# Layer norms by statistics operations, one tile at a time, and a staggered context norm

## The chip, the cores and the metric

The kernel runs on one core of a Trainium2 chip. The metric is the device time of one execution in microseconds. The kernel before was run three times: 4507.76, 4507.40 and 4503.47 us, with a median of 4507.4 us.

## The reference

Two layers of a gated cross-attention network on a residual `x` of 1024 rows of 128 features, with a context of 6404 rows of 128. Each layer adds a gated cross-attention and a gated mixture of eight experts. What matters for this change is where rows are normalised:

```python
def _layernorm(x, axis=-1, eps=1e-05):
    m = jnp.mean(x, axis=axis, keepdims=True)
    v = jnp.var(x, axis=axis, keepdims=True)
    return (x - m) / jnp.sqrt(v + eps)

# layer 0, cross-attention: context and latents are normalised once more inside
xn = layernorm(x, ln_x_g, ln_x_b)         # x here is the context, 6404 rows
ln = layernorm(latents, ln_l_g, ln_l_b)   # latents = _layernorm(residual)
# layer 1, cross-attention: the input and the output go through
def stable_layernorm(x, g):
    x = x / jax.lax.stop_gradient(jnp.max(x, axis=-1, keepdims=True))
    mean = jnp.mean(x, axis=-1, keepdims=True)
    var = jnp.mean(jnp.square(x - mean), axis=-1, keepdims=True)
    return (x - mean) * jax.lax.rsqrt(var + EPS) * g

x = x + tanh(g_xattn[0]) * xattn0(ctx, _layernorm(x))
x = x + tanh(g_ffn[0]) * experts0(_layernorm(x))
x = x + tanh(g_xattn[1]) * xattn1(_layernorm(x), ctx)
x = x + tanh(g_ffn[1]) * experts1(_layernorm(x))
```

## The kernel before

Rows lie on the 128 partitions, so the residual `X` is a tile of 128 x 8 x 128 (QT = 8 tiles of 128 rows), and the context `raw` (in the trace `a_ctx_rows`) is 128 x 51 x 128: 50 full tiles and one of 4 rows. A layer norm is then a reduction along the free axis within each partition. The program is a chain of blocks; every engine meets the others at the end of a block.

`layer_norm` (lines 119 to 130) handles T tiles at once on VectorE: a sum (L122), its division (L123), a subtraction of the mean with a broadcast operand (L124), a square (L125), a second sum (L126) and variance plus epsilon (L127). GpSimd raises that to the power -0.5 (`rstd`, L135), and VectorE multiplies by the result (L130). Each of these waits for the one before it through the semaphore `ln_step` or through the pair `var_ready` and `rstd_ready`. It is called for eight tiles in seven places: twice in the preparation of each attention layer, once behind the second attention, once in each mixture. Three more calls norm the context of layer 0, in parts of 17 tiles (`ln_parts`).

**The preparation of layer 0** is the block of lines 255 to 425. SyncE loads the context (L259, L261, semaphore `c_in`). VectorE norms the latents twice, tells TensorE by `lat_ready`, waits for the context (L359), then norms the three parts, with one `ctx_ready` behind each (L361 to L364). The rows are transposed in 16 jobs of up to four tiles: two for the latents, four for the tiles that need only the first part, four that need the second, six that need the third (the last two of these are of two tiles and of one). For each job TensorE transposes (L421), ScalarE applies gain and bias into `xt`, which has two buffers (L302, trace `a_x_new`), and copies to the rounded `hi` (L305, `a_x_hi`), and GpSimd subtracts to get `lo` (L330, `a_x_lo`). ScalarE may start job i only when `lo` of job i - 2 is done. GpSimd's queue is in a fixed order: it does the powers and the `lo` work by the calls of lines 332 to 340,

```python
rstd(pool, 17, var_ready, rstd_ready, 3)
lows(0, 2)
rstd(pool, 17, var_ready, rstd_ready, 4)
lows(2, 6)
rstd(pool, 17, var_ready, rstd_ready, 5)
lows(6, len(jobs))
```

The block ends when GpSimd's last `lo` is done; the next one begins with GpSimd's fills (L561 to L563).

**The preparation of layer 1** is the same code with another `hi` and `lo` path: ScalarE writes `hi` (L308), VectorE writes `lo` (L384, L387), and the context isn't normalised. VectorE norms the latents, divides by the row maximum (L354 to L356) and norms again. TensorE's jobs for the context wait for the same transfer `c_in` (L416).

**The mixtures** (`moe_layer`) begin with a layer norm of X (L1348), then TensorE transposes (L1392), ScalarE copies, and TensorE computes the gate's logits (L1397) once the expert weights are loaded (`w_in`, L1395). The wait at L1420 counts the steps of the norm.

The rest, about nine tenths of the span, is the main loops of the two attentions, which the change doesn't touch.

## Time and profile before

| | |
|---|---|
| the profiled execution's own time | 4508.5 us |
| span in its profile | 4506.7 us |
| runs | 4503.47, 4507.40, 4507.76 us |
| TensorE busy | 4199.3 us, 93% of the span |
| VectorE busy | 3411.4 us, 76% |
| ScalarE busy | 3192.4 us, 71% |
| GpSimd busy | 414.8 us, 9% |

The span is cut into stages by the blocks: preparation of layer 0 up to 86.2 us, the start of its attention to about 130 us, its loop to about 2300 us, the first mixture from 2322 to 2466 us, preparation of layer 1 to 2534 us, its loop to about 4428 us, the end of that attention to 4446 us and the second mixture to the end. Only the stretches outside the two loops contain layer norms. In them the engines wait for each other in turn, so that a timeline of one engine with its idle times tells which one the others wait for.

### The profile page before, as it was taken

How to read it: one execution, taken by the hardware profiler on the slowest of the kernel's cores; microseconds unless marked ns; L12 is line 12 of the kernel's file. 1: busy time of each engine (PE TensorE's matmuls, PEld its weight loads, DVE VectorE, ACT ScalarE, POOL GpSimd, SP SyncE). 2: the span in 40 equal slices, each digit the busy share in tenths (PEclk: the TensorE clock that was granted, in tenths of full speed). 3: DMA queues.
4: the chain of work that ended last, by engine and by line, in shares of the span. 5: the costliest groups of instructions: out<-in, count | busy, mean ns of one | idle time of the engine just before them, and what ended most of it. 6: DMA issues, size and time to landing. Idle time of an engine off the chain costs nothing. (4 is left out here: it accounts for less than half of the span.)

```text
span 4506.7 us, 75798 instructions
## 1 busy us (share of the span) xinstructions
PE 4199.3 (93%) x26651; PEld 2695.9 (60%) x26651; DVE 3411.4 (76%) x5067; ACT 3192.4 (71%) x5163; POOL 414.8 (9%) x348
## 2 busy tenths in 40 slices
PE   2999999999999999999978499999999999999995
PEld 1556666666666656666646366666666666666663
DVE  5788878787887888788752577777777777777785
ACT  2788888888888888888842367676766666666661
POOL 4111111111111111111100000000000000000000
PEclk9999999999999999999989599999999999999996
DMA  1000000000000000000010000000000000000000
GB/s 36 16 1 16 1 5 12 1 16 1 17 1 1 16 1 17 1 5 12 1 51 25 26 3 14 3 5 12 5 12 5 12 5 12 2 15 1 16 1 23
DMA packets 27285, 48.16 MB, mean 11 GB/s; under 512 B 9329, under 2 KB 18425, under 8 KB 24313
## 3 DMA queue, kind: packets, MB, share of 16 engines
q1 hardware_dynamic: 24824, 42.30, 2.8%
q8 instruction: 237, 3.88, 0.4%
q14 instruction: 158, 1.29, 0.1%
q10 hardware_dynamic: 2066, 0.69, 0.1%
HBM read 42.15 MB, written 0.82 MB: 10 GB/s over the span
## 5 line engine op out<-in xcount | busy, mean ns | idle before, releaser
L797 DVE TENSOR_TENSOR a_probs_lo<-a_probs 128x1024 fp32r<-128x1024 f32 x1764 | 2119.5, 1223 | 656.8 <-ACT a_probs L642 306.8
L638 ACT ACTIVATE a_probs<-scores_ps,a_c_bias,a_k_rstd 128x512 f32<-128x512 f32 x1892 | 1317.2, 776 | 35.9 <-PE scores_ps L1114 34.4
L1139 PE MATMUL out_ps<-a_probs_lo,a_v 128*128 128x512 f32 x3520 | 1135.6, 443 | 0.0
L1132 PE MATMUL out_ps<-a_probs,a_v 128*128 128x512 bf16 x3520 | 968.7, 391 | 37.7 <-DVE a_out_acc L810 27.7
L642 ACT ACTIVATE a_probs<-scores_ps,a_c_bias 128x1024 f32<-128x1024 f32 x818 | 870.4, 1112 | 115.6 <-PE scores_ps L1114 114.6
L1114 PE MATMUL scores_ps<-a_q_hi,a_k_hi 64*128 64x512 f32 x3528 | 793.6, 445 | 18.3 <-issue 9.4
L1139 PEld LDWEIGHTS out_ps<-a_probs_lo,a_v 128*128 128x128 f32 x3520 | 659.2, 188 | 220.4 <-issue 0.3
L1114 PE MATMUL scores_ps<-a_q_lo,a_k_hi 64*128 64x512 f32 x3528 | 703.4, 393 | 0.0
L1114 PE MATMUL scores_ps<-a_q_hi,a_k_lo 64*128 64x512 f32 x3528 | 699.2, 391 | 0.0
L1132 PEld LDWEIGHTS out_ps<-a_probs,a_v 128*128 128x128 f16 x3520 | 273.8, 97 | 590.8 <-issue 222.9
L607 ACT ACTIVATE a_v<-proj_ps 128x256 f16<-128x256 f32 x456 | 175.5, 385 | 519.2 <-PE proj_ps L1049 519.0
L1114 PEld LDWEIGHTS scores_ps<-a_q_hi,a_k_hi 64*128 64x128 f32 x3528 | 333.2, 184 | 209.1 <-issue 109.6
L569 POOL TENSOR_TENSOR a_k_rstd<-a_k_stat,minus_half 128x4 f32<-128x4 f32 x244 | 301.5, 1236 | 1698.5 <-DVE a_k_stat L774 1698.5
L1114 PEld LDWEIGHTS scores_ps<-a_q_lo,a_k_hi 64*128 64x128 f32 x3528 | 336.0, 185 | 76.0
L810 DVE TENSOR_TENSOR a_out_acc<-out_ps,a_out_acc 128x512 f32<-128x512 f32 x576 | 369.1, 682 | 11.4 <-PE out_ps L1139 11.4
L1114 PEld LDWEIGHTS scores_ps<-a_q_hi,a_k_lo 64*128 64x128 f32 x3528 | 335.6, 186 | 37.5
L618 ACT ACTIVATE a_k_hi<-proj_ps 128x256 fp32r<-128x256 f32 x454 | 175.2, 386 | 248.6 <-PE proj_ps L1057 248.1
L624 ACT ACTIVATE a_v<-a_v 128x512 fp32r<-128x512 f16 x454 | 283.9, 625 | 0.0
L1122 PE MATMUL spare_ps<-a_probs,a_v_last 128*32 128x512 bf16 x3520 | 283.1, 395 | 0.0
L1049 PE MATMUL proj_ps<-a_wkv_hi,a_x_hi 128*128 128x256 f32 x912 | 267.4, 293 | 14.7 <-ACT normed_T L675 6.9
L1049 PE MATMUL proj_ps<-a_wkv_lo,a_x_hi 128*128 128x256 f32 x912 | 258.9, 284 | 0.0
L1049 PE MATMUL proj_ps<-a_wkv_hi,a_x_lo 128*128 128x256 f32 x912 | 257.0, 282 | 0.0
(198 smaller groups left out, 3431.1 us busy)
## 6 DMA issues: line engine op xcount, KB each, us to landing
a_den<-a_inv_row SPq DMA_DIRECT2D x18, 1024.0 KB, 4.7
normed<-in_L_xattn_we_g SPq DMA_DIRECT2D x18, 256.0 KB, 2.8
a_wkv_raw<-in_L_xattn_wkv_g SPq DMA_DIRECT2D x18, 128.0 KB, 2.0
a_wo_raw<-in_L_xattn_wo_g SPq DMA_DIRECT2D x18, 128.0 KB, 2.0
m_w<-in_L_ffn_w1T SPq DMA_DIRECT2D x1, 2048.0 KB, 8.2
m_w<-in_L_ffn_w2T SPq DMA_DIRECT2D x1, 2048.0 KB, 12.6
a_wq_raw<-in_L_xattn_wq_g SPq DMA_DIRECT2D x18, 64.0 KB, 1.9
residual<-in_x SPq DMA_DIRECT2D x1, 512.0 KB, 3.8
```

Of the source, the lines that this page charges most:

```text
L569: nc.gpsimd.tensor_tensor(krs[:, par, 2 * j:2 * j + 2, :].rearrange("p t h -> p (t h)"), kst[:, 1, :], mhalf[:, 0:2 * GH], ALU.pow).then_i ...
L607: nc.scalar.activation(v16[:, par, 2 * j:2 * j + 2, :, 0:DH].rearrange("p t h d -> p (t h) d"), proj[:, 2 * P:4 * P].rearrange("p (a d) -> ...
L624: nc.scalar.activation(v32[:, par, 2 * j:2 * j + 2, :, :].rearrange("p t h k -> p (t h) k"), v16[:, par, 2 * j:2 * j + 2, :, :].rearrange( ...
L638: ins = nc.scalar.activation(probs[:, pb, e * 512:(e + 1) * 512], scores[:, b, e * 512:(e + 1) * 512], ACT.Exp, bias=cbias[:, tile:tile + ...
L642: ins = nc.scalar.activation(probs[:, pb, :], scores[:, b, :], ACT.Exp, bias=cbias[:, 1:2] if last else cbias[:, 0:1])
L797: nc.vector.tensor_tensor(plow[:, idx % NPL, :], probs[:, idx % NB, :], p_hi[:, idx % NB], ALU.subtract).then_inc(plo_ready, 1)
L810: ins = nc.vector.tensor_tensor(oacc[:, e, q], outs[:, e * 512:(e + 1) * 512], oacc[:, e, q], ALU.add)
L1049: last = nc.tensor.matmul(dst, a[:, x], w[:, :].rearrange("p (a c) -> p a c", a=2), start=t == 0 and m == 0, stop=m == 2, skip_group_check ...
L1114: last = nc.tensor.matmul(scores[:, b, e * 512:(e + 1) * 512], kk[r, c % 2, t, :], qq[r, n * 512:(n + 1) * 512], start=m == 0, stop=m == 2)
L1122: last = nc.tensor.matmul(last_ps[j:j + 32, :], vlast[:, c % 2, t, e, 4 - 4 * n:36 - 4 * n], p_hi[:, idx % NB, e * 512:(e + 1) * 512], sta ...
L1132: nc.tensor.matmul(outs[:, e * 512:(e + 1) * 512], v16[:, c % 2, t, e, :], p_hi[:, idx % NB, e * 512:(e + 1) * 512], start=t == 0, stop=False)
L1139: nc.tensor.matmul(outs[:, e * 512:(e + 1) * 512], v32[:, c % 2, t, e, :], plow[:, idx % NPL, e * 512:(e + 1) * 512], start=False, stop=t ...
```

## The change

Per tile, `bn_stats` gives six statistics of 128 values, `bn_aggr` makes mean and variance of them, and one `tensor_scalar` with two per-partition scalars subtracts the mean and multiplies by the power. The statistics lie in `few`, a part of `squares`, or for the context in `part`, a part of `a_ctx_sq`. `layer_norm` is now `ln_stats` followed by `ln_apply`. For the context the two are called apart: the statistics of part i + 1 come ahead of the application to part i. GpSimd's order changes with that: the second power comes ahead of the latents' two jobs, the third right behind them.

```diff
-        def layer_norm(dve, step, x, dst, sq, T, var_ready, rstd_ready, n):
-            shape = [P, T, D]
-            step(nc.vector.tensor_reduce(stat[:, 0, 0:T], x, AX.X, ALU.add))
-            step(nc.vector.tensor_scalar(stat[:, 1, 0:T], stat[:, 0, 0:T], 1.0 / D, None, ALU.mult))
-            step(nc.vector.tensor_tensor(dst, x, over(stat[:, 1, 0:T], shape), ALU.subtract))
-            step(nc.vector.tensor_tensor(sq, dst, dst, ALU.mult))
-            step(nc.vector.tensor_reduce(stat[:, 2, 0:T], sq, AX.X, ALU.add))
-            nc.vector.tensor_scalar(stat[:, 3, 0:T], stat[:, 2, 0:T], 1.0 / D, LN_EPS,
-                                    ALU.mult, ALU.add).then_inc(var_ready, 1)
-            dve.wait_ge(rstd_ready, n)
-            step(nc.vector.tensor_tensor(dst, dst, over(stat[:, 0, 0:T], shape), ALU.mult))
+        few = sqz[:, :, :].rearrange("p t d -> p (t d)")[:, 0:8 * QT].rearrange("p (t k) -> p t k", k=8)
+
+        def ln_stats(dve, step, x, a, b, part, var_ready):
+            for t in range(a, b):
+                nc.vector.bn_stats(part[:, t, 0:6], x[:, t, :]).then_inc(step.sem, 1)
+            step.n += b - a
+            dve.wait_ge(step.sem, step.base + step.n)
+            for t in range(a, b):
+                nc.vector.bn_aggr(part[:, t, 6:8], part[:, t, 0:6]).then_inc(step.sem, 1)
+            step.n += b - a
+            dve.wait_ge(step.sem, step.base + step.n)
+            nc.vector.tensor_scalar(stat[:, 3, a:b], part[:, a:b, 7], LN_EPS, None, ALU.add).then_inc(var_ready, 1)
+
+        def ln_apply(dve, step, x, dst, a, b, part, rstd_ready, n):
+            dve.wait_ge(rstd_ready, n)
+            for t in range(a, b):
+                nc.vector.tensor_scalar(dst[:, t, :], x[:, t, :], part[:, t, 6:7], stat[:, 0, t:t + 1],
+                                        ALU.subtract, ALU.mult).then_inc(step.sem, 1)
+            step.n += b - a
+            dve.wait_ge(step.sem, step.base + step.n)
+
+        def layer_norm(dve, step, x, dst, T, var_ready, rstd_ready, n):
+            ln_stats(dve, step, x, 0, T, few, var_ready)
+            ln_apply(dve, step, x, dst, 0, T, few, rstd_ready, n)
...
                     if L == 0:
-                        rstd(pool, 17, var_ready, rstd_ready, 3)
+                        rstd(pool, 17, var_ready, rstd_ready, 3, 0)
+                        rstd(pool, 17, var_ready, rstd_ready, 4, 17)
                         lows(0, 2)
-                        rstd(pool, 17, var_ready, rstd_ready, 4)
-                        lows(2, 6)
-                        rstd(pool, 17, var_ready, rstd_ready, 5)
-                        lows(6, len(jobs))
+                        rstd(pool, 17, var_ready, rstd_ready, 5, 34)
+                        lows(2, len(jobs))
...
                     if L == 0:
+                        part = sq[:, :, :].rearrange("p t d -> p (t d)")[:, 0:(CTX_FULL + 1) * 8].rearrange("p (t k) -> p t k", k=8)
+                        def normed(i):
+                            a, b = ln_parts[i]
+                            ln_apply(dve, step, raw, raw, a, b, part, rstd_ready, 3 + i)
+                            dve.sem_inc(ctx_ready, 1)
                         for i, (a, b) in enumerate(ln_parts):
-                            layer_norm(dve, step, raw[:, a:b, :], raw[:, a:b, :], sq[:, 0:b - a, :], b - a,
-                                       var_ready, rstd_ready, 3 + i)
-                            dve.sem_inc(ctx_ready, 1)
+                            ln_stats(dve, step, raw, a, b, part, var_ready)
+                            if i:
+                                normed(i - 1)
+                        normed(len(ln_parts) - 1)
...
-                                pe.wait_ge(step_s, 6 + 1)
+                                pe.wait_ge(step_s, 3 * QT + 1)
```

VectorE in the preparation of layer 0, the context's part of the order before; `stat` holds sums, means, variances and powers:

```order
L122 TENSOR_REDUCE stat<-a_ctx_rows 128x17 [waits a0_ln_step,a0_ctx_in]
L123 TENSOR_SCALAR stat<-stat 128x17 [waits a0_ln_step]
L124 TENSOR_TENSOR a_ctx_rows<-a_ctx_rows,stat 128x2176 [waits a0_ln_step]
L125 TENSOR_TENSOR a_ctx_sq<-a_ctx_rows 128x2176 [waits a0_ln_step]
L126 TENSOR_REDUCE stat<-a_ctx_sq 128x17 [waits a0_ln_step]
L127 TENSOR_SCALAR stat<-stat 128x17 [waits a0_ln_step]
L130 TENSOR_TENSOR a_ctx_rows<-a_ctx_rows,stat 128x2176 [waits a0_rstd_ready]
L122 TENSOR_REDUCE stat<-a_ctx_rows 128x17 [waits a0_ln_step]
```

and what stands there now:

```order
L124 BN_STATS a_ctx_sq<-a_ctx_rows 128x6 [waits a0_ln_step,a0_ctx_in]
L124 BN_STATS a_ctx_sq<-a_ctx_rows 128x6 x16
L128 BN_AGGR a_ctx_sq<-a_ctx_sq 128x2 [waits a0_ln_step]
L128 BN_AGGR a_ctx_sq<-a_ctx_sq 128x2 x16
L131 TENSOR_SCALAR stat<-a_ctx_sq 128x17 [waits a0_ln_step]
L124 BN_STATS a_ctx_sq<-a_ctx_rows 128x6 x17
L128 BN_AGGR a_ctx_sq<-a_ctx_sq 128x2 [waits a0_ln_step]
L128 BN_AGGR a_ctx_sq<-a_ctx_sq 128x2 x16
L131 TENSOR_SCALAR stat<-a_ctx_sq 128x17 [waits a0_ln_step]
L137 TENSOR_SCALAR a_ctx_rows<-a_ctx_rows,a_ctx_sq,stat 128x128 [waits a0_rstd_ready]
L137 TENSOR_SCALAR a_ctx_rows<-a_ctx_rows,a_ctx_sq,stat 128x128 x16
```

The application to the first part (L137) now stands behind the statistics of the second, and only the first instruction of each group waits.

GpSimd in the same block before (`a_x_lo` is the `lo` of a job):

```order
L135 TENSOR_TENSOR stat<-stat,minus_half 128x17 [waits a0_var_ready]
L330 TENSOR_TENSOR a_x_lo<-a_x_new,a_x_hi 128x512 [waits a0_xh_done] x2
L135 TENSOR_TENSOR stat<-stat,minus_half 128x17 [waits a0_var_ready]
L330 TENSOR_TENSOR a_x_lo<-a_x_new,a_x_hi 128x512 [waits a0_xh_done] x4
L135 TENSOR_TENSOR stat<-stat,minus_half 128x17 [waits a0_var_ready]
L330 TENSOR_TENSOR a_x_lo<-a_x_new,a_x_hi 128x512 [waits a0_xh_done] x8
```

and now:

```order
L149 TENSOR_TENSOR stat<-stat,minus_half 128x17 [waits a0_var_ready] x2
L344 TENSOR_TENSOR a_x_lo<-a_x_new,a_x_hi 128x512 [waits a0_xh_done] x2
L149 TENSOR_TENSOR stat<-stat,minus_half 128x17 [waits a0_var_ready]
L344 TENSOR_TENSOR a_x_lo<-a_x_new,a_x_hi 128x512 [waits a0_xh_done] x12
L344 TENSOR_TENSOR a_x_lo<-a_x_new,a_x_hi 128x256 [waits a0_xh_done]
```

All work on the context's jobs now stands behind the third power; before, four jobs stood ahead of it.

## Rows read from the trace of the kernel before

**Rows 1.** The page's busy part, the whole span: engine, busy us, share, instructions

```profile
PE 4199.3 (93%) x26651; PEld 2695.9 (60%) x26651; DVE 3411.4 (76%) x5067; ACT 3192.4 (71%) x5163; POOL 414.8 (9%) x348
```

**Rows 2.** Windows: stretch, its us, busy us (instructions), PEclk, DMA share, GB/s

```profile
0.00:91.50 91.50, 16.22 (x60) 10.93 (x60) 59.00 (x47) 23.00 (x37) 43.18 (x39) 1.00 0.17 45
...
200.00:700.00 500.00, 488.92 (x3146) 308.33 (x3145) 405.36 (x614) 424.24 (x747) 78.15 (x61) 1.00 0.02 8
```

**Rows 3.** Timeline of VectorE, the first layer norm: start us, us, operation [idle before]

```profile
6.24 1.22 DVE L122 TENSOR_REDUCE stat<-residual 128x8 f32<-128x1024 f32 x1 [6.24 <-PEq L97]
...
11.49 0.17 DVE L127 TENSOR_SCALAR stat<-stat 128x8 f32<-128x8 f32 x1
...
13.51 1.23 DVE L130 TENSOR_TENSOR normed<-normed,stat 128x1024 f32<-128x1024 f32 x1 [1.85 <-POOL stat L135]
...
14.77 1.22 DVE L122 TENSOR_REDUCE stat<-normed 128x8 f32<-128x1024 f32 x1
```

**Rows 4.** VectorE on the context: the first reductions, ns min/median/max, and the last operation's timeline row

```profile
L122 DVE TENSOR_REDUCE stat<-a_ctx_rows x3: 2421/2421/2421, 23.3 to 57.3; 128x17 f32<-128x2176 f32 x3
...
71.73 3.47 DVE L130 TENSOR_TENSOR a_ctx_rows<-a_ctx_rows,stat 128x2176 f32<-128x2176 f32 x1 [3.18 <-POOL stat L135]
```

**Rows 5.** Timeline of GpSimd in the first stage's second half

```profile
53.63 5.94 POOL L330 TENSOR_TENSOR a_x_lo<-a_x_new,a_x_hi 128x512 fp32r<-128x512 f32 x3
...
68.64 3.06 POOL L135 TENSOR_TENSOR stat<-stat,minus_half 128x17 f32<-128x17 f32 x1 [7.49 <-DVE stat L127]
...
77.91 2.61 POOL L330 TENSOR_TENSOR a_x_lo<-a_x_new,a_x_hi 128x512 fp32r<-128x512 f32 x2 [0.33 <-ACT a_x_hi L305]
...
83.57 1.95 POOL L330 TENSOR_TENSOR a_x_lo<-a_x_new,a_x_hi 128x512 fp32r<-128x512 f32 x2 [0.23 <-ACT a_x_hi L305]
...
85.75 0.45 POOL L330 TENSOR_TENSOR a_x_lo<-a_x_new,a_x_hi 128x128 fp32r<-128x128 f32 x1 [0.23 <-ACT a_x_hi L305]
```

**Rows 6.** Windows at the end of the two context transfers, columns as in rows 2

```profile
20.50:21.00 0.50, 0.00 (x0) 0.00 (x0) 0.00 (x0) 0.00 (x0) 0.50 (x1) 1.00 0.23 55
...
21.00:21.50 0.50, 0.00 (x0) 0.00 (x0) 0.00 (x0) 0.00 (x0) 0.50 (x1) 1.00 0.01 4
...
2483.00:2483.50 0.50, 0.00 (x0) 0.00 (x0) 0.30 (x2) 0.00 (x0) 0.09 (x1) 0.50 0.30 95
...
2485.00:2486.00 1.00, 0.00 (x0) 0.00 (x0) 0.92 (x1) 0.00 (x0) 0.05 (x1) 0.50 0.04 12
```

**Rows 7.** Timeline of VectorE, small operations and one that reads one tensor

```profile
90.75 0.29 DVE L815 TENSOR_TENSOR a_wkv_lo<-a_wkv_raw,a_wkv_hi 128x128 fp32r<-128x128 f32 x1 [0.58 <-ACT a_wkv_hi L649]
...
90.96 0.29 DVE L816 SCALAR_TENSOR_TENSOR a_wkv_lo<-a_wkv_raw,a_wkv_hi 128x128 fp32r<-128x128 f32 x1
...
4461.94 0.64 DVE L1353 MAX8 m_top<-m_logit 128x8 f32<-128x8 f32 x8
...
4468.84 1.12 DVE L1382 SCALAR_TENSOR_TENSOR residual<-proj_ps,m_combine,residual 128x128 f32<-128x128 f32 x4 [2.15 <-PE proj_ps L1427]
...
2317.77 0.75 DVE L1244 TENSOR_SCALAR branch<-branch,a_cols 128x1024 f32<-128x1024 f32 x1 [0.32 <-PEq L508]
...
84.95 0.62 DVE L374 TENSOR_SCALAR a_rows<-a_rows 128x64 f32<-128x64 f32 x1
```

**Rows 8.** One line's instructions in the main loop: ns min/median/max

```profile
L797 DVE TENSOR_TENSOR a_probs_lo<-a_probs x1764: 1207/1225/1295, 128.7 to 4405.6; 128x1024 fp32r<-128x1024 f32 x196
```

**Rows 9.** Timeline of TensorE after the first layer's mixture norm

```profile
2336.26 0.99 PE L1397 MATMUL proj_ps<-m_wg,normed_T 128*128 128x8 f32 x4 [3.08 <-DMA m_w<-in_L_ffn_w2T]
```

**Rows 10.** Timeline of TensorE, transposes of the second layer's preparation

```profile
2486.42 1.97 PE L421 MATMUL scores_ps<-identity,normed 128*128 128x128 f32 x8 [12.01 <-DVEq L358]
...
2489.29 1.09 PE L421 MATMUL scores_ps<-identity,a_ctx_rows 128*128 128x128 f32 x4 [0.91 <-DVE a_ln_lo L384]
```

**Rows 11.** The last norm: a window as in rows 2, and TensorE's row

```profile
4450.00:4451.00 1.00, 0.00 (x0) 0.00 (x0) 0.97 (x2) 0.00 (x0) 0.00 (x0) 0.50 0.00 0
...
4458.07 3.58 PE L1397 MATMUL proj_ps<-m_wg,normed_T 128*128 128x8 f32 x16 [1.11 <-ACT normed_T L1333]
```

More of the change, by code:

```diff
@@ L132, in rstd @@
-        def rstd(pool, T, var_ready, rstd_ready, n):
+        few = sqz[:, :, :].rearrange("p t d -> p (t d)")[:, 0:8 * QT].rearrange("p (t k) -> p t k", k=8)
[9 more added lines that the diff above has]
+            nc.vector.tensor_scalar(stat[:, 3, a:b], part[:, a:b, 7], LN_EPS, None, ALU.add).then_inc(var_ready, 1)
@@ L134, in rstd @@
+        def rstd(pool, T, var_ready, rstd_ready, n, a=0):
             pool.wait_ge(var_ready, n)
-            nc.gpsimd.tensor_tensor(stat[:, 0, 0:T], stat[:, 3, 0:T], mhalf[:, 0:T],
+            nc.gpsimd.tensor_tensor(stat[:, 0, a:a + T], stat[:, 3, a:a + T], mhalf[:, 0:T],
                                     ALU.pow).then_inc(rstd_ready, 1)
@@ L350, in _ @@
                     step = Steps(dve, ln_step)
-                    layer_norm(dve, step, X[:, :, :], Z[:, :, :], sqz[:, :, :], QT, var_ready, rstd_ready, 1)
+                    layer_norm(dve, step, X, Z, QT, var_ready, rstd_ready, 1)
                     if L == 1:
@@ L356, in _ @@
                         step(nc.vector.tensor_tensor(Z[:, :, :], Z[:, :, :], over(stat[:, 1, 0:QT], [P, QT, D]), ALU.mult))
-                    layer_norm(dve, step, Z[:, :, :], Z[:, :, :], sqz[:, :, :], QT, var_ready, rstd_ready, 2)
+                    layer_norm(dve, step, Z, Z, QT, var_ready, rstd_ready, 2)
                     dve.sem_inc(lat_ready, 1)
```

8 lines of the change are left out of this document (4 added, 4 removed).

## The prediction

> **What bounds the kernel now.** The busy part of the page comes first [rows 1]: TensorE is at 93%, so in most of the span a faster VectorE can bring nothing. The windows then show where that doesn't hold [rows 2]: in 500 us of a main loop TensorE is busy for 489, in the first 91.5 us for 16, with VectorE at 59. Layer norms lie only in such stretches. So the question for each norm is whether VectorE ends the wait there. I read that from the timelines, norm by norm.
>
> A norm of eight tiles takes 14.77 - 6.24 = 8.53 us [rows 3]: five large operations of 1.22, two small ones of 0.17 to 0.19, 1.85 of waiting for GpSimd's power, and about 0.03 between operations. The other six run alike, at about 8.45. In the first layer's preparation the context's part starts at 23.3, ends at 71.73 + 3.47 = 75.20 [rows 4], and the stage ends with GpSimd's last `lo` at 86.20 [rows 5]. Whatever ends that `lo` earlier shifts all that follows.
>
> **The price of the new operations.** No row shows a statistics operation, so I bound each by the nearest rows [rows 7].
> - BN_STATS reads 128 columns of one tensor. Two independent operations of 128 columns start 0.21 apart and last 0.29. I take 0.21 for each and 0.29 for the last. Ends: 0.15 if it used a second read port, 0.34 if the program passed twice over the 128 columns (0.21 plus 128/1024 of about 1.07, the share of 1.22 that grows with the columns).
> - BN_AGGR reads six numbers. MAX8 on eight columns takes 0.64 for eight, 0.08 each. I take that, since it's the row with about as many columns. Ends: 0.05, and 0.17, which a lone small operation like L127 lasts [rows 3].
> - The new TENSOR_SCALAR has one SBUF tensor as input. L1244, of that form, takes 0.75 for 1024 columns where two-input operations take 1.22 [rows 3], so for 128 columns it saves about 0.06: 0.15 apart, 0.25 for the last. Ends: 0.08 (MAX8) and 0.26 (L1382, four in 1.12).
>
> Here a rule speaks against the change. In the trace, L816 starts 0.21 after L815, which lasts 0.29: independent operations overlap, which many small ones need [rows 7]. The Trainium skill (VectorE: DVE Perf Modes, The DRAIN you can't avoid) says that an operation does not start until the pipe of the one before is empty, and advises few operations; the trace disagrees for independent ones. What it would give here is the first rival.
>
> **A norm of eight tiles afterwards.** Statistics 7 x 0.21 + 0.29 = 1.76; aggregation 0.64; the addition of epsilon 0.17; two gaps 0.08; the way to GpSimd and back about 1.80, unchanged; application 7 x 0.15 + 0.25 = 1.30; gap 0.03. Sum 5.78, so 2.7 less than 8.45.
>
> **Part by part, against the profiled execution's own 4508.5 us.**
> 1. *Latents of layer 0.* The two norms end at 6.24 + 2 x 5.78 = 17.8 instead of about 23.2. But VectorE then needs the context, and its transfer still moves 55 GB/s up to 21.0 and 4 behind that [rows 6]. I take 20.9. Three microseconds of the gain turn into a wait for the transfer.
> 2. *Context of layer 0.* For 17 tiles: statistics 16 x 0.21 + 0.29 = 3.65, aggregation 17 x 0.08 = 1.36, epsilon 0.18, gaps 0.11, in all 5.3. The third `var_ready` of the context comes behind three such groups and one application (16 x 0.15 + 0.25 + 0.05 = 2.7), at 20.9 + 15.9 + 2.7 = 39.5. The first two powers lie under statistics; the third, 3.06 plus 0.08 to start [rows 5], doesn't, and all `lo` work of the context is queued behind it. It starts at 42.6. From 77.91 to 83.57 GpSimd starts four full `lo`, 1.415 each, paced together with ScalarE and its two buffers, and from the start of the last full one to the end there are 86.20 - 83.57 = 2.63 [rows 5]. Twelve full jobs: 42.6 + 11 x 1.415 + 2.63 = 60.8.
> 3. *The shared port.* The application to the last part runs beside `lo` work. The trace shows that this hurts: L374, a one-input operation on 64 columns, takes 0.62 beside a `lo`, twice what L815 needs for 128 [rows 7], and L130 on the context 3.47 where the operations of the same size take 2.42 [rows 4]. Statistics should be spared, since the third reduction, at 57.3 beside `lo` work, kept the 2.42 of the other two [rows 4, 5]. If the 17 applications and the `lo` simply exclude each other, GpSimd loses up to 17 x 0.15 = 2.6, some of it in pauses that it has anyway; I take half, 1.3. The stage ends at 62.1 instead of 86.2: **24.1 us**.
> 4. *Mixture of layer 0.* After its norm TensorE waits 3.08 us for the expert weights [rows 9], and their transfer starts with the block. A norm shorter by 2.7 only lengthens that wait: **0**. If this cover were missing, it would be 2.7 more.
> 5. *Preparation of layer 1.* Two norms, 5.4. The latents' transposes move from 2486.42 to 2481.0 and the context's from 2489.29 to 2483.9 [rows 10]; the context's transfer is thinning out by then, 95 GB/s at 2483 and 12 at 2485 [rows 6]. Between a loss of 0 and of 2 I take 0.4, since little is left at 2483.5: **5.0**.
> 6. *Norm behind the second attention.* Nothing beside it: **2.7**.
> 7. *Mixture of layer 1.* Its weights have landed before 4450 (0 GB/s in that window), and TensorE needs them at 4458.07 - 2.7, measured against a block that starts earlier by as much [rows 11]: **2.7**.
>
> Sum 24.1 + 0 + 5.0 + 2.7 + 2.7 = 34.5, so 4508.5 - 34.5 = 4474.0; the median shown lies 1.1 below the profiled execution, hence 4472.9, rounded to **4473**.
>
> **Rivals.**
> - *Small operations don't overlap.* Each pays its whole length: 0.29, 0.17 and 0.25 per tile. The eight-tile norm takes 7.75 and gains 0.7; the latents end at 21.7; a context part takes 17 x 0.46 + 0.29 = 8.1, an application 4.3, the third `var_ready` comes at 50.3, the power ends at 53.5 and the stage, by the 19.5 from there of part by part 2 and 3, at 73.0. Gain 13.2 + 1.4 + 0.7 + 0.7 = 16.0: 4491. For it: statistics operations may be built otherwise than MAX8. Against it: L815 and L816 overlap, and so do eight MAX8 in 0.64. Chance 0.13.
> - *GpSimd starves the last application.* The Trainium skill (SBUF — State Buffer, SBUF: two separate sides) calls the port an exclusive lock held for the whole instruction; L374 and L130 agree [rows 4, 7]. Worked out from rows: if one application gets through per `lo` and a third in the pause of each pair, 12 are done when eight `lo` are (42.6 + 8 x 1.415 = 53.9), the rest at 54.7. From VectorE's last context operation to the end of the stage were 86.20 - 75.20 = 11.0, so it ends at 65.7 instead of 62.1: gain 30.9, time 4476.5. Chance 0.12. The powers don't act so: L797 never exceeds 1295 ns among 1764, though GpSimd's powers run among them [rows 8].
> - *Slower.* The statistics operation is a long program, several passes over the tile at a slow rate. On the path lie 51 tiles of the context and 32 of the later norms, 83 in all. The gain of 34.5 is used up at 0.42 more per tile, that is where statistics and aggregation together cost 0.71 instead of 0.29. At 0.85 they add 46 there and some 6 more in the latents, past the wait: 18 slower, 4525. Against it: the rows on 128 columns last 0.29, and four of L1382 take 1.12. Chance 0.03.
> - *The gain is taken back.* Everything behind the first stage shifts by 24 us; something that doesn't shift (a transfer, TensorE's granted clock at the start of a loop) eats most of it. The loops' loads are issued inside them and shift too. Chance 0.03, about 4500.
>
> **How the numbers follow.** The forecast has 0.69. Its own spread: statistics at 0.15 give 83 x 0.06 = 5 more, no port loss 1.3 and no late transfer 0.4, thus 4466; statistics at 0.26, aggregation at 0.10 and applications at 0.20 cost 4.2 + 1.7 + 2.5 = 8.4, thus 4481. The starved case lies inside; the range reaches to the first rival's 4491 and down to 4465. A measurement here tells 0.2%, 9 us, from no change: all three first cases are faster by more. Faster 0.94, same 0.03, slower 0.03.
>
> **What would show it.** In the profile afterwards: BN_STATS groups of 17 lasting 3.7 us and BN_AGGR groups 1.4; VectorE idle for about 3 us before the context, released by the transfer; one power between statistics and the `lo` run, which starts near 42 and ends near 62; applications of 2.6 us for parts one and two and a much longer one for part three; the wait for the expert weights in the first mixture grown to 5.8; the norms at 5.8 elsewhere. BN_STATS lasting 0.4 or more each, a stage end behind 70, or loops that are longer than before would make the forecast wrong.

## The result, and the profile after

The changed kernel takes 4482.4 us (median of six runs, 4479.22 to 4483.43) where the kernel before takes 4506.8 (median of six, 4503.47 to 4507.76): a ratio of 0.9946, with a 95% interval from 0.9936 to 0.9956. The gain by medians is 24.4 us; 34.5 were forecast. The changed kernel's profiled execution took 4479.22, 3.2 below its median, and that of before 4508.5, 1.7 above its median, so 4.9 of the 29.3 by which the two profiles differ belong to these two executions and not to the change.

The page's busy part, beside [rows 1]:

```profile
PE 4194.4 (94%) x26651; PEld 2692.1 (60%) x26651; DVE 3394.0 (76%) x5328; ACT 3191.6 (71%) x5163; POOL 408.7 (9%) x348
```

VectorE is busy for 17 us less and TensorE for 5 less: most of what shrank is time in which TensorE waited.

VectorE's timeline (start us, us, operation, idle time before it) begins with one norm of eight tiles, which answers to [rows 3], and then shows the context's three parts, which answer to [rows 4]:

```profile
6.25 1.65 DVE L124 BATCH_NORM_STATS2 squares<-residual 128x6 f32<-128x128 f32 x8 [6.25 <-PEq L97]
7.93 0.64 DVE L128 BATCH_NORM_AGGREGATE squares<-squares 128x2 f32<-128x6 f32 x8
...
10.63 2.14 DVE L137 TENSOR_SCALAR normed<-residual,squares,stat 128x128 f32<-128x128 f32 x8 [1.86 <-POOL stat L149]
12.80 1.64 DVE L124 BATCH_NORM_STATS2 squares<-normed 128x6 f32<-128x128 f32 x8
```

```profile
21.90 3.38 DVE L124 BATCH_NORM_STATS2 a_ctx_sq<-a_ctx_rows 128x6 f32<-128x128 f32 x17 [2.67 <-DMA a_ctx_rows<-in_ctx]
25.32 1.23 DVE L128 BATCH_NORM_AGGREGATE a_ctx_sq<-a_ctx_sq 128x2 f32<-128x6 f32 x17
...
31.44 6.47 DVE L137 TENSOR_SCALAR a_ctx_rows<-a_ctx_rows,a_ctx_sq,stat 128x128 f32<-128x128 f32 x17
38.06 3.39 DVE L124 BATCH_NORM_STATS2 a_ctx_sq<-a_ctx_rows 128x6 f32<-128x128 f32 x17
...
42.84 7.56 DVE L137 TENSOR_SCALAR a_ctx_rows<-a_ctx_rows,a_ctx_sq,stat 128x128 f32<-128x128 f32 x17
50.55 9.48 DVE L137 TENSOR_SCALAR a_ctx_rows<-a_ctx_rows,a_ctx_sq,stat 128x128 f32<-128x128 f32 x17 [0.15 <-DVE a_ctx_rows L137]
```

A norm takes 12.80 - 6.25 = 6.55 us, where it took 8.53. Its statistics and aggregation cost what was expected (1.65 and 0.64), its application 2.14 instead of 1.30. The context starts at 21.90, behind a wait of 2.67 for the transfer. Statistics of 17 tiles take 3.38 and aggregation 1.23, but the same 17 applications take 6.47, then 7.56, then 9.48.

GpSimd beside them, to compare with [rows 5]:

```profile
34.67 2.65 POOL L344 TENSOR_TENSOR a_x_lo<-a_x_new,a_x_hi 128x512 fp32r<-128x512 f32 x2
43.00 3.12 POOL L149 TENSOR_TENSOR stat<-stat,minus_half 128x17 f32<-128x17 f32 x1 [5.68 <-DVE stat L131]
46.06 2.70 POOL L344 TENSOR_TENSOR a_x_lo<-a_x_new,a_x_hi 128x512 fp32r<-128x512 f32 x2
...
53.24 2.61 POOL L344 TENSOR_TENSOR a_x_lo<-a_x_new,a_x_hi 128x512 fp32r<-128x512 f32 x2 [1.58 <-ACT a_x_hi L319]
...
62.88 2.60 POOL L344 TENSOR_TENSOR a_x_lo<-a_x_new,a_x_hi 128x512 fp32r<-128x512 f32 x2 [4.21 <-ACT a_x_hi L319]
...
69.21 0.46 POOL L344 TENSOR_TENSOR a_x_lo<-a_x_new,a_x_hi 128x128 fp32r<-128x128 f32 x1 [0.23 <-ACT a_x_hi L319]
```

The third power starts at 43.00 (39.6 was forecast), the `lo` run behind it at 46.06 (42.6), and the stage ends at 69.67 (62.1) instead of 86.20. In the run there are two pauses that the forecast didn't have, 1.58 and 4.21. ScalarE's and TensorE's rows for the second pause:

```profile
61.36 0.78 ACT L316 ACTIVATE a_x_new<-scores_ps,a_cols 128x512 f32<-128x512 f32 x1 [4.03 <-PE scores_ps L442]
```

```profile
60.14 1.97 PE L442 MATMUL scores_ps<-identity,a_ctx_rows 128*128 128x128 f32 x8 [5.08 <-DVEq L379]
```

The transposes for part three wait for VectorE's last application, which ended at 60.03. Behind the first stage two rows answer to [rows 9] and to the norms elsewhere:

```profile
2316.60 3.55 PE L1418 MATMUL proj_ps<-m_wg,normed_T 128*128 128x8 f32 x16 [5.23 <-DMA m_w<-in_L_ffn_w2T]
```

```profile
4410.74 1.64 DVE L124 BATCH_NORM_STATS2 squares<-normed 128x6 f32<-128x128 f32 x8
...
4417.21 1.23 DVE L1280 TENSOR_TENSOR normed<-normed,a_rows 128x1024 f32<-128x1024 f32 x1
```

TensorE's wait for the expert weights grew from 3.08 to 5.23, and the norm behind the second attention takes 4417.21 - 4410.74 = 6.47 instead of about 8.45.

The stages against each other, in us (the first loop begins with VectorE's fill of `spare_ps`, here called the loop's start):

| stage | before | after | gain | forecast |
|---|---|---|---|---|
| preparation of layer 0, to the loop's start | 89.6 | 73.1 | 16.5 | 24.1 |
| loop's start to the first mixture | 2233.1 | 2229.8 | 3.3 | 0 |
| first mixture | 144.0 | 145.2 | -1.2 | 0 |
| preparation of layer 1, to its loop | 71.1 | 67.6 | 3.5 | 5.0 |
| second loop, with the norm behind it | 1908.7 | 1904.7 | 4.0 | 2.7 |
| second mixture | 60.2 | 57.1 | 3.1 | 2.7 |

The gains add up to the spans' difference, 29.3, within rounding. Of the last two the norms themselves account for 2.0 each. The first row is far above scatter: a second profile of the changed kernel (e11 below) has 73.07. The preparation of layer 1 is clear of it too (71.1 and in e2 71.3 with the old operations, 67.2 to 69.3 in all kernels with the new statistics). In the loops and mixtures kernels that share their code differ by 2 to 4 us, as much as the gains shown there.

### The profile page after: what moved, and what is told of

It is laid out like the page before. It is cut to its first block and busy times, and to the rows that moved or that the text cites. A ratio compares the mean times of both kernels' runs of the same rounds, so it can differ in the third digit from the quotient of the medians.

```text
span 4477.4 us, 76059 instructions
## 1 busy us (share of the span) xinstructions
PE 4194.4 (94%) x26651; PEld 2692.1 (60%) x26651; DVE 3394.0 (76%) x5328; ACT 3191.6 (71%) x5163; POOL 408.7 (9%) x348
## 3 DMA queue, kind: packets, MB, share of 16 engines
q14 instruction: 163, 1.33, 0.1%
```

## Experiments

All stage times come from each kernel's one profiled execution; medians of the whole kernel scatter by some 2 us. What separates the variants is the loop's start: 89.63 before, 73.10 after. The first theory: the forecast's mechanism holds, and what it missed is one price (the application) and one contention (`lo` against application). The rivals: the order brings the gain by itself, or the operations do; the loops changed.

**The change's two halves (e1, e2).** In e1 the order is the old one:

```diff
                         for i, (a, b) in enumerate(ln_parts):
                             ln_stats(dve, step, raw, a, b, part, var_ready)
-                            if i:
-                                normed(i - 1)
-                        normed(len(ln_parts) - 1)
+                            normed(i)
```

with GpSimd's calls as before (power, `lows(0, 2)`, power, `lows(2, 6)`, power, `lows(6, ...)`).

> The new operations everywhere, but the context's three parts one after the other as in the kernel before (statistics, power, application of a part before the next part's statistics; the `lo` work between the powers). Theory A (the shortfall lies in the application's own cost of 0.257 us per tile, and in the `lo` work that starves it): a part takes 4.8 for statistics, 3.2 for the power and 4.5 for the application; parts end at 34.4, 46.9 and, since the third power waits for four `lo`, about 60 to 62; six full `lo` are left after the third power, two of which can run beside the application, so the preparation ends at 69 to 71, where the changed kernel has 69.7: the stagger by itself is worth about nothing. Whole kernel within 3 us of the changed one, about 4483. Rival B (the stagger carries the gain, as 'all lo work behind one power' was forecast to end at 62): without it three powers of 3.1 stand open instead of one, the preparation ends at 76 or later, and the kernel takes about 4490.

It took 4492.4 us (six runs; ratio to before 0.997, 0.9957 to 0.9982). The last `lo` ended at 79.02, the loop started at 82.45: rival B. VectorE's rows show why:

```profile
29.68 6.36 DVE L137 TENSOR_SCALAR a_ctx_rows<-a_ctx_rows,a_ctx_sq,stat 128x128 f32<-128x128 f32 x17 [3.17 <-POOL stat L149]
...
44.23 8.48 DVE L137 TENSOR_SCALAR a_ctx_rows<-a_ctx_rows,a_ctx_sq,stat 128x128 f32<-128x128 f32 x17 [3.17 <-POOL stat L149]
...
60.90 8.48 DVE L137 TENSOR_SCALAR a_ctx_rows<-a_ctx_rows,a_ctx_sq,stat 128x128 f32<-128x128 f32 x17 [3.17 <-POOL stat L149]
```

Each application stands behind an open power (3.17), and the two later ones have four `lo` beside them and take 8.48. I had let them run free.

The kernel e2 has the old operations in the new order (`ln_stats` with two reductions, division, subtraction and square of 17 tiles, `ln_apply` with one wide product).

> The old operations (reductions and wide two-input operations) in the new, staggered order. Theory A: statistics of a part 10.3, so parts at 33.6 and 43.9, application 2.4 or more, third variance at about 57 to 59, third power until 60 to 63, ten full `lo` behind it: 60.1 + 9 x 1.415 + 2.63 = 75.5 to 78; 8 to 11 less than the 86.2 of before, so 4496 to 4499 in all, nothing gained elsewhere. Rival B (order is worth nothing by itself with either kind of operation): preparation at 84 to 87, kernel 4505 to 4508.

4501.9 us (ten runs; ratio 0.999, 0.998 to 1.0), last `lo` at 82.57, loop's start at 86.00, between the two forecasts. The order alone gives 3.6 us, the operations alone 7.2, both together 16.5. GpSimd's rows show what lies between 75.5 and 82.57:

```profile
33.55 3.06 POOL L144 TENSOR_TENSOR stat<-stat,minus_half 128x17 f32<-128x17 f32 x1 [11.70 <-DVE stat L130]
43.66 5.17 POOL L144 TENSOR_TENSOR stat<-stat,minus_half 128x17 f32<-128x17 f32 x1 [7.05 <-DVE stat L130]
48.80 6.87 POOL L339 TENSOR_TENSOR a_x_lo<-a_x_new,a_x_hi 128x512 fp32r<-128x512 f32 x2
57.29 5.16 POOL L144 TENSOR_TENSOR stat<-stat,minus_half 128x17 f32<-128x17 f32 x1 [1.62 <-DVE stat L130]
62.42 5.88 POOL L339 TENSOR_TENSOR a_x_lo<-a_x_new,a_x_hi 128x512 fp32r<-128x512 f32 x3
```

The same power takes 3.06 beside VectorE's reduction and 5.17 beside wide two-input operations; two `lo` take 6.87 instead of 2.5. So the third power ends at 62.45, where the lower forecast had 60.1 (2.3 us), and the first three `lo` behind it take 5.88 beside the last wide application instead of 3.9 (2.0). The rest, 2.8, is a slip of the expectation: it counted ten full `lo` behind the third power, and in this order there are twelve. Staggering lays the powers beside wide operations, unless the operations are replaced too; that explains at least part of why the halves add up to less than the whole.

**What a `lo` does to an application (e3).**

```diff
                         rstd(pool, 17, var_ready, rstd_ready, 5, 34)
+                        pool.wait_ge(ctx_ready, 3)
                         lows(2, len(jobs))
```

> The changed kernel, but GpSimd's `lo` work from the third on waits until VectorE has ended the last application. Theory A (a `lo` holds VectorE's operations back): the second and third application take 4.5 each (0.257 x 17 + 0.1), as the first does where no `lo` runs, instead of 7.56 and 9.48; the third ends near 55, and the preparation ends at about 55 + 9 x 1.415 + 2.63 = 70 or a bit more, since ten `lo` follow. Rival (the later applications are slow for another reason, such as operands written by GpSimd or a slower VectorE): they still take 7 to 9 and the preparation ends at 74 or later.

```profile
31.22 6.48 DVE L137 TENSOR_SCALAR a_ctx_rows<-a_ctx_rows,a_ctx_sq,stat 128x128 f32<-128x128 f32 x17
...
42.62 4.44 DVE L137 TENSOR_SCALAR a_ctx_rows<-a_ctx_rows,a_ctx_sq,stat 128x128 f32<-128x128 f32 x17
47.20 4.44 DVE L137 TENSOR_SCALAR a_ctx_rows<-a_ctx_rows,a_ctx_sq,stat 128x128 f32<-128x128 f32 x17
```

Theory A: the second and third application take 4.44, and the first, which still has two `lo` beside it, 6.48. The last `lo` ended at 69.88, so to hold the `lo` work back gains nothing over letting it starve the applications: what the applications win, the `lo` work loses, as it waits for them. The 70 of the expectation was met by luck: the third application ended at 51.64 instead of near 55, and twelve full `lo` follow it instead of ten, 51.78 + 11 x 1.415 + 2.63 = 70.0. One run: 4485.8 us. Windows of the changed kernel say it in small: stretch, its us, the busy us and number of applications that lie in it at least in part, PEclk, DMA share, GB/s.

```profile
33.50:34.60 1.10, 1.10 (x6) 1.00 0.00 0
34.70:36.00 1.30, 1.30 (x2) 1.00 0.00 0
34.86:36.04 1.18, 1.18 (x1) 1.00 0.00 0
51.70:53.20 1.50, 1.50 (x8) 1.00 0.00 0
```

The counts take in those that an edge of the window cuts. Beside a power (until 34.67) the applications go on at their own pace, 0.256 apart, as in the pause from 51.66. From 34.86 to 36.04, beside one `lo`, a single one lies open; the second of the row above had started before the `lo` and was ending. So one application gets through per `lo`, 1.28 after the one before instead of 0.256, and is open for the length of the `lo`, the longest 1411 ns. Each `lo` beside applications costs them 1.28 - 0.256 = 1.02 us, and that gives the lengths of the groups: 4.44 + 2 x 1.02 = 6.48 for the first (6.47 measured), three `lo` 7.5 (7.56), five 9.5 (9.48), and four in e1 8.5 (8.48).

**The price of the application (e4).** The mean and the power are replaced by two constants, so this kernel leaves the normalisation's subtraction and factor out:

```diff
-                nc.vector.tensor_scalar(dst[:, t, :], x[:, t, :], part[:, t, 6:7], stat[:, 0, t:t + 1],
+                nc.vector.tensor_scalar(dst[:, t, :], x[:, t, :], 0.01, 0.99,
                                         ALU.subtract, ALU.mult).then_inc(step.sem, 1)
```

> The application in every norm with two constants instead of the tile's mean and power read from memory: the mean's subtraction and the power's factor are left out of the result. Theory A1 (0.257 apart is the price of the two scalars read from memory before the columns): with constants the operations start 0.15 to 0.20 apart and last 0.25 to 0.29, the eight-tile application takes 1.3 to 1.6 instead of 2.14, and each later norm is 0.5 to 0.9 shorter. Rival A2 (the price is that of any one-input, two-operation instruction on 128 columns in float32): still 0.25 apart, 2.1 for eight.

```profile
10.56 1.17 DVE L137 TENSOR_SCALAR normed<-residual 128x128 f32<-128x128 f32 x8 [1.85 <-POOL stat L149]
...
31.52 2.40 DVE L137 TENSOR_SCALAR a_ctx_rows<-a_ctx_rows 128x128 f32<-128x128 f32 x17
...
42.15 9.94 DVE L137 TENSOR_SCALAR a_ctx_rows<-a_ctx_rows 128x128 f32<-128x128 f32 x17 [0.89 <-POOL stat L149]
```

```profile
39.01 3.10 POOL L149 TENSOR_TENSOR stat<-stat,minus_half 128x17 f32<-128x17 f32 x1 [1.74 <-DVE stat L131]
...
61.25 0.46 POOL L344 TENSOR_TENSOR a_x_lo<-a_x_new,a_x_hi 128x128 fp32r<-128x128 f32 x1 [0.22 <-ACT a_x_hi L319]
```

Eight take 1.17 and seventeen 2.40, hence (2.40 - 1.17) / 9 = 0.137 apart, where the real ones take (4.44 - 2.14) / 9 = 0.256: reading two scalars per partition from memory costs 0.12 us per instruction here. That is A1, below even its 0.15 to 0.20, and it shows more: with an application near the 0.15 that the forecast had taken, the third power ends at 42.1 (42.6 forecast) and the stage at 61.7 (62.1 forecast). One run: 4472.3 us (4473 forecast). The third application still took 9.94 beside `lo` work, so whether an application is held off has nothing to do with its scalars. But here the second application had ended at 41.25, before the `lo` run began; only one stands beside it instead of two. From the third power's end to the last `lo` the stage needs 19.6; in e3, with no application beside the `lo` run, it needs 69.88 - 51.78 = 18.1. One starved application thus costs the end 1.5.

**The application by wide operations (e5).**

```diff
-            for t in range(a, b):
-                nc.vector.tensor_scalar(...)
+            step(nc.vector.tensor_tensor(dst[:, a:b, :], x[:, a:b, :], over(part[:, a:b, 6], shape), ALU.subtract))
+            step(nc.vector.tensor_tensor(dst[:, a:b, :], dst[:, a:b, :], over(stat[:, 0, a:b], shape), ALU.mult))
```

> The application of every norm as two wide two-input operations (subtract the means, multiply by the powers) in place of one operation per tile; statistics and order as in the change. Theory A (per-tile operations with two scalars cost 0.257 each, wide ones 1.22 per eight tiles and 2.42 per 17): the eight-tile application takes 2.5 instead of 2.14, so each of the four later norms is 0.3 to 0.4 longer; 17 tiles take 4.9 where no `lo` runs instead of 4.45. Beside `lo` a wide operation was held by about 1 us only (3.47 for 2.42), where 17 small ones take 7.6 to 9.5: so the second and third application take 5 to 7, and the preparation ends at 66 to 69 instead of 69.7; whole kernel the same within 2 us. Rival B (one instruction per tile is the better form even beside `lo`): the preparation ends at 70 to 74 and the kernel is 2 to 5 slower than the changed one.

```profile
46.53 3.47 DVE L137 TENSOR_TENSOR a_ctx_rows<-a_ctx_rows,a_ctx_sq 128x2176 f32<-128x2176 f32 x1 [0.49 <-POOL stat L147]
50.04 3.37 DVE L138 TENSOR_TENSOR a_ctx_rows<-a_ctx_rows,stat 128x2176 f32<-128x2176 f32 x1
```

```profile
31.53 5.17 POOL L147 TENSOR_TENSOR stat<-stat,minus_half 128x17 f32<-128x17 f32 x1 [1.71 <-DVE stat L131]
...
41.33 5.17 POOL L147 TENSOR_TENSOR stat<-stat,minus_half 128x17 f32<-128x17 f32 x1 [2.14 <-DVE stat L131]
46.47 9.28 POOL L342 TENSOR_TENSOR a_x_lo<-a_x_new,a_x_hi 128x512 fp32r<-128x512 f32 x4
```

4484.1 us (four runs), the last `lo` at 68.54: theory A, 1.1 earlier than in the change, which the median doesn't show. Two instructions lose one stretch of about 1 us each to a `lo`, where seventeen lose many; in return both powers beside the wide operations take 5.17, and four `lo` 9.28. Wide operations and `lo` hold each other off. With the power it is one-sided: beside the second power (31.53 to 36.70) a wide operation runs from 33.82 to 36.25 in its usual 2.42, while the power waits.

**The order once more (e6).** All three statistics ahead of all applications; on GpSimd the latents' two `lo`, then three powers, then the rest:

> All three statistics of the context first, then the three applications; on GpSimd the two `lo` of the latents before the first power, then the three powers, then all `lo` of the context. Theory A (the loss in the changed kernel is that the third part's tiles are applied last, after the third power, and beside `lo` work that starves them, so ScalarE waits 4.0 for part three): statistics end at 36.2, the third power at 39.3, the first application runs free until 40.8, GpSimd's context work starts near 43.9 and is never without input again, twelve full `lo` later the preparation ends at 61.5 to 64. Kernel 4474 to 4477. Rival B (VectorE and GpSimd share one port and the work on it is what counts, whatever the order): the preparation ends at 67 or later. Rival C (statistics first is worse, since the first `lo` of the context starts 0 to 3 later): 70.

```profile
36.18 4.44 DVE L137 TENSOR_SCALAR a_ctx_rows<-a_ctx_rows,a_ctx_sq,stat 128x128 f32<-128x128 f32 x17
40.77 8.60 DVE L137 TENSOR_SCALAR a_ctx_rows<-a_ctx_rows,a_ctx_sq,stat 128x128 f32<-128x128 f32 x17 [0.15 <-DVE a_ctx_rows L137]
49.52 8.60 DVE L137 TENSOR_SCALAR a_ctx_rows<-a_ctx_rows,a_ctx_sq,stat 128x128 f32<-128x128 f32 x17 [0.15 <-DVE a_ctx_rows L137]
```

4479.7 us (four runs), the last `lo` at 67.76: rival B, and theory A's 61.5 to 64 failed. The first application is free (4.44), the other two take 8.60 each; GpSimd stood still twice for 3.18, before 52.21 and 60.97. What it gained over the change, 1.9, is about what e10 gets by moving the latents' `lo` alone; the rest of the order only moves the loss about.

**The `lo` subtractions on VectorE (e7)**, between its own operations (`lows_v(0, 2)` behind the second statistics, `lows_v(2, 4)` behind the second application, the rest at the end), GpSimd with the powers alone:

> The first preparation's `lo` subtractions on VectorE instead of GpSimd, placed between its statistics and applications; GpSimd has only the powers. Theory A (applications are slow because a GpSimd `lo` holds VectorE off): all three applications take 4.4 to 4.5; a `lo` of 512 columns takes VectorE 0.6 to 0.7; the third application ends at 52.5, and from there ScalarE's two activations per job (1.33) set the pace: end at 64 to 66, 4 to 6 less than in the change. Rival B (applications slow in themselves from the second on): 7.6 and 9.5 again, end at 72 or later.

```profile
32.56 4.44 DVE L137 TENSOR_SCALAR a_ctx_rows<-a_ctx_rows,a_ctx_sq,stat 128x128 f32<-128x128 f32 x17
...
47.72 4.44 DVE L137 TENSOR_SCALAR a_ctx_rows<-a_ctx_rows,a_ctx_sq,stat 128x128 f32<-128x128 f32 x17
...
54.50 0.69 DVE L383 TENSOR_TENSOR a_x_lo<-a_x_new,a_x_hi 128x512 fp32r<-128x512 f32 x1 [0.91 <-ACT a_x_hi L319]
...
65.39 0.29 DVE L383 TENSOR_TENSOR a_x_lo<-a_x_new,a_x_hi 128x128 fp32r<-128x128 f32 x1 [0.26 <-ACT a_x_hi L319]
```

Theory A in each number: applications of 4.44, `lo` of 0.69 (GpSimd needs 1.3), ScalarE's pace of 1.33 from 54.50 on, the end at 65.68. The loop's start moved only from 73.10 to 70.83, since the small operations on `a_rows` and `a_cols`, which had stood under cover of GpSimd's work, now come behind the last `lo`; the median of four runs, 4482.1, shows no gain.

**The transfer (e8)**, in layer 0 alone; layer 1 keeps its one transfer and its wait:

```diff
-                    sp.dma_start(raw[:, 0:CTX_FULL, :], ...).then_inc(c_in, 16)
+                    for s, (a, b) in zip((c_first, c_second, c_in), ((0, 17), (17, 34), (34, CTX_FULL))):
+                        sp.dma_start(raw[:, a:b, :], ...).then_inc(s, 16)
...
-                    dve.wait_ge(c_in, 32)
...
+                            dve.wait_ge(*((c_first, 16), (c_second, 16), (c_in, 32))[i])
                             ln_stats(dve, step, raw, a, b, part, var_ready)
```

> The context's transfer of layer 0 in three transfers with a semaphore each, so that VectorE's statistics of part one wait for part one alone. Theory A (the 2.67 us that VectorE waits for the transfer lie on the path): statistics start at 19.2 to 19.4, everything behind moves by 2.5, the preparation ends at 67.0 to 67.5, kernel 2.5 less than the changed one. Rival B (the parts land together, since the queues work on all of them at once, or later parts then come late): the first part lands at 21 or later, the end is within 1 of 69.7.

```profile
19.38 3.38 DVE L124 BATCH_NORM_STATS2 a_ctx_sq<-a_ctx_rows 128x6 f32<-128x128 f32 x17
```

The statistics follow the latents' norm without a wait, the last `lo` ends at 67.10, and the median of four runs is 4478.6: theory A.

**One move (e10).** GpSimd's latents' `lo` ahead of the first power:

```diff
+                        lows(0, 2)
                         rstd(pool, 17, var_ready, rstd_ready, 3, 0)
                         rstd(pool, 17, var_ready, rstd_ready, 4, 17)
-                        lows(0, 2)
                         rstd(pool, 17, var_ready, rstd_ready, 5, 34)
```

> The changed kernel with one thing moved: GpSimd does the two `lo` of the latents before the context's first power instead of after the second. Theory A (a `lo` beside an application costs what the applications lose): the first application, with no `lo` beside it, takes 4.44 instead of 6.47, the third statistics, the third power and the second application start 2.0 earlier, and the preparation ends 1.5 to 2.0 earlier: last `lo` at 67.7 to 68.2. Rival B (the two `lo` only stand elsewhere in the same chain, since from the second application on GpSimd's `lo` and the applications exclude each other and the sum is the same): end within 0.5 of 69.7.

```profile
31.33 4.45 DVE L137 TENSOR_SCALAR a_ctx_rows<-a_ctx_rows,a_ctx_sq,stat 128x128 f32<-128x128 f32 x17
```

The first application takes 4.45, all behind it comes 2.1 earlier, the last `lo` ends at 67.54, and the kernel takes 4478.4 us (five runs): theory A, a little more than its 67.7 to 68.2. So a `lo` beside statistics cost nothing, and beside an application it cost 1.0.

**All together (e9, e9b).** The transfer in parts, the latents' `lo` first, three statistics, and then, for every group of four tiles, its applications and VectorE's own `lo` of the group two before:

```diff
+                        for i in range(2, len(jobs)):
+                            a, b = jobs[i][1][0], jobs[i][1][-1] + 1
+                            dve.wait_ge(rstd_ready, 2 + sum(b > c for c, d in ln_parts))
+                            for t in range(a, b):
+                                ins = nc.vector.tensor_scalar(raw[:, t, :], raw[:, t, :], part[:, t, 6:7], stat[:, 0, t:t + 1],
+                                                              ALU.subtract, ALU.mult)
+                                ins.then_inc(step.sem, 1)
+                            step.n += b - a
+                            dve.wait_ge(step.sem, step.base + step.n)
+                            dve.sem_inc(ctx_ready, 1)
+                            if i >= 4:
+                                low_v(i - 2)
...
-                            pe.wait_ge(ctx_ready, 1 + sum(tiles[-1] >= b for a, b in ln_parts))
+                            pe.wait_ge(ctx_ready, i - 1)
```

The small operations on rows and columns went ahead of the last `lo`.

> All that helped, put together: the context's transfer in three parts, the latents' two `lo` on GpSimd first, all three statistics, then the applications by groups of four tiles (one job of the transposes each) with the context's `lo` subtractions between them on VectorE, two groups behind. Theory (VectorE's own work is then the bound, with no operation stretched): 19.4 + 3 x 4.78 = 33.7, then 51 applications and 13 drains of about 0.12 (14.8) and 12 `lo` of 0.66 with two short ones (8.7): last `lo` at 57 to 60, first instruction of the loop (VectorE's memset) at 61 to 64 where the changed kernel has 73.1; kernel 9 to 12 less than the changed one, 4471 to 4474. Rival (ScalarE's two activations per job, 1.33, or their two buffers become the bound, with the `lo` waiting for them): last `lo` at 62 or later.

4474.0 us (five runs; ratio 0.9927, 0.9913 to 0.994), the last `lo` at 60.03, at the upper end of the theory, the loop's start at 63.56. In the second form a group's last application signals `ctx_ready` itself, and the wait for `step.sem` goes:

> As e9_interleaved, but a group's last application signals TensorE itself, and VectorE goes on without waiting for it. If the bound is VectorE's own work, 13 waits of about 0.1 go: 1.0 to 1.5 earlier than e9_interleaved. If ScalarE paces the groups, no difference.

```profile
38.56 1.11 DVE L400 TENSOR_SCALAR a_ctx_rows<-a_ctx_rows,a_ctx_sq,stat 128x128 f32<-128x128 f32 x4
39.59 0.69 DVE L394 TENSOR_TENSOR a_x_lo<-a_x_new,a_x_hi 128x512 fp32r<-128x512 f32 x1
...
57.74 0.29 DVE L394 TENSOR_TENSOR a_x_lo<-a_x_new,a_x_hi 128x128 fp32r<-128x128 f32 x1
```

```profile
34.10:58.10 24.00, 13.82 (x52) 8.65 (x52) 22.28 (x73) 18.10 (x28) 3.09 (x1) 0.66 0.00 1
```

4472.1 us (five runs; ratio to before 0.9925, 0.9912 to 0.9939), 10 less than the change by medians; the loop starts at 61.56, 11.5 earlier than in the change. Between the third statistics and the end VectorE is busy for 22.28 of 24.00 us (the third column of busy times, behind TensorE's two), so it is the bound, and no operation is stretched. The 13 waits cost 2.0, more than the 1.0 to 1.5 that were expected.

**The change again (e11).**

> The changed kernel itself once more. Theory (the profiled execution's main loops were short by chance: its first loop took 2229.8 us where the kernel before had 2233.1, and the seven variants run so far that keep these loops as they are had 2228.0 to 2232.3): the preparation ends at 69.7 within 0.3 again, so that this part of the difference is the change's own, while the first loop's length comes out anywhere from 2228 to 2233; median 4480 to 4484. Rival (the loops are shorter because of the change): 2229.8 within 0.3 again.

4481.5 us (five runs); the last `lo` at 69.64, the first loop 2230.21 long, the first mixture 143.72. The loop's length came out near the first time's 2229.77, though outside the 0.3 that the rival gave; this run by itself doesn't tell the two apart. All profiles taken together do in part: kernels with the change's operations had first loops of 2228.0 to 2232.3, with nothing in their preparation that orders them (e3, nearly the changed kernel, 2232.3; e1 2228.0), and the one with the old operations 2231.7. Of before there is one profile, 2233.1. So a scatter of 4 us between kernels is shown; a small part of the 3.3 that the change itself would have caused isn't excluded. The mixture's 145.2 in the first profile was chance as well: ten of the experiments' twelve values lie from 143.5 to 144.1, with either kind of norm, and the kernel before has 144.0.

## Why the prediction was right, and where it wasn't

- *What bounds the kernel, and where the gain lies.* Right: only the stretches outside the loops changed, and 16.5 of the gain lie in the first stage.
- *The price of the new operations.* Statistics: 0.21 apart forecast, (3.38 - 1.65) / 9 = 0.19 measured; aggregation as forecast (0.64 for eight). **The application is the mis-sized term**: 0.15 apart forecast, 0.256 measured. The upper end kept for it, 0.26 by L1382 [rows 7], was exact, and that row was the nearest: 128 columns and a scalar per partition read from memory. I had taken the 0.21 between two-input operations and subtracted what L1244 saves over 1024 columns, in which a cost per instruction doesn't show. The constants of e4 give that cost, 0.12, and with an application near the forecast's price the stage ends where the forecast had it; the late start of the context (1.0) and the cheaper statistics (1.6) nearly cancel in that.
- *Part 1, latents.* The gain does turn into a wait, of 2.67 instead of 3; the context starts at 21.90 instead of 20.9. The transfer's last bytes by the windows [rows 6] aren't yet the moment at which VectorE starts.
- *Part 2, the chain to the third power.* Its `var_ready` was forecast for 39.5, and the power starts at 43.00, so 3.4 late after its 0.08 to start: 1.0 from the start, -1.6 from three statistics of 4.78 instead of 5.3, 3.9 from the first application (6.62 with its wait at the end, instead of 2.7). Of these 3.9, some 1.9 are the application's own price (4.45 without a `lo`, and 0.15) and 2.0 the two latents' `lo` beside it, which the part didn't consider; e10 took these 2.0 away. The forecast's own sign, applications of 2.6 for parts one and two, failed with 6.47 and 7.56.
- *Part 3, the shared port.* Taken at 1.3 for the last application alone. The stretch from the third power's end to the stage's end took 69.67 - 46.06 = 23.6 instead of 19.5, so 4.1 more, and 5.5 more than the 18.1 of e3, where every part is ready and nothing contends. The rival *GpSimd starves the last application* had 23.1 for it (65.7 - 42.6), and its rule, one application per `lo`, is what the trace shows. That its sum came so near is in part luck: it took the last application to start with the `lo` run, while that starts at 50.55, behind a second application that is starved too. Part three is ready 60.03 - 46.06 = 14.0 behind the power instead of 12.1, and the stage ends 9.6 after that instead of 11.0. The contention isn't a cost apart from the price: e4, whose third application is starved as much, needs 19.6 from the third power's end, as forecast, since its second application was over by then. In the change the dearer applications are late, so two of them meet the `lo` run, and parts two and three reach TensorE late. The stage end of 69.67 lies just inside the 70 that the forecast had named as a sign against itself. That statistics are spared was right: 3.37 to 3.39 for 17 wherever they stood. So was the reading of L374: with no `lo` beside it the same operation takes 0.20 in e9b.
- *Part 4, first mixture.* Right: TensorE waits 5.23 instead of 3.08 for the expert weights, and with the old norm (e2) and the new one (e11) the mixture takes 143.8 and 143.7.
- *Parts 5 to 7.* Right in kind: the preparation of layer 1 gives 3.5 instead of 5.0 (its two norms 3.9 instead of 5.4), and the other two norms 2.0 each instead of 2.7. The second mixture as a whole gave 3.1 in this profile and 1.0 in the repeat's (59.2 us).
- *The sum.* With measured terms 16.5 + 0 + 3.5 + 2.0 + 2.0 = 24.0, against 24.4 by medians, so the loops needn't have given anything; with the preparation of layer 1 uncertain by 2 us, that agreement is no sharper than this. Of 34.5 forecast, 7.6 are missing in the first stage and 2.9 in the later norms.
- *The rival "small operations don't overlap"* is out. Statistics of 276 ns each start 0.19 apart. It was built on one half of what the Trainium skill states (VectorE: DVE Perf Modes, The DRAIN you can't avoid): the section also says that a next operation that is not held starts earlier. The trace agrees with that other half for these independent operations.

## What to carry to other kernels

Price a small operation by a row with the same number of columns and the same kind of operands; a long row of the same opcode hides what each instruction costs. Before two engines are staggered, list which instructions of theirs will lie beside each other after the move: here `lo` beside applications (2.0 us at the first one, more behind the third power) took back part of what the order won, with the old operations the powers beside wide ones did the same, and laying `lo` beside statistics, or doing it on VectorE itself, cost nothing or little. Try operations and order together before either is dropped for bringing little: the halves gave 3.6 and 7.2, the whole 16.5.

## What the runs showed of the hardware

- A `lo` (GpSimd, two SBUF tensors) and some VectorE operations exclude each other by whole instructions. It holds off TENSOR_SCALAR on 128 float32 columns, with scalars from memory or constants (longest 1411 and 1306 ns instead of 340 and 213, one through per `lo`), and wide two-input operations (3.47 for 2.42), and wide two-input operations hold off a `lo` (two take 6.87 instead of 2.5). Two `lo` beside small applications take 2.65 to 2.70 instead of 2.60, so those hardly delay it. BN_STATS is held off by nothing (3.37 to 3.39 for 17 in all profiles). The Trainium skill (SBUF — State Buffer, SBUF: two separate sides) names a lock for the whole instruction between GpSimd and those VectorE operations that use both ports or read two SBUF tensors. The trace agrees for `lo`.
- The power is held off by wide two-input operations (5.17 for 3.06) and doesn't hold VectorE off: beside it applications stay 0.256 apart and the wide operation of e5 takes its 2.42. For the power the trace agrees with that lock in one direction only.
- Two operand scalars per partition cost 0.12 us per instruction on 128 columns: 0.256 against 0.137 apart, and 340 against 213 ns long (e4).
- BN_STATS on 128 float32 columns: 276 ns, 0.19 apart; BN_AGGR on its six numbers: 147 to 149 ns (medians), 0.07 apart.
